# Moving the last group's norm over six stage joints and weight rounding one stage ahead

## The reference

```python
def _layernorm(x, axis=-1, eps=1e-05):
    m = jnp.mean(x, axis=axis, keepdims=True)
    v = jnp.var(x, axis=axis, keepdims=True)
    return (x - m) / jnp.sqrt(v + eps)
...
x = x + jnp.tanh(g_xattn[0]) * _L0_xattn_ref(_layernorm(x, axis=-1), ctx_1024, ctx_1024, ...)
x = x + jnp.tanh(g_ffn[0]) * _L0_ffn_ref(_layernorm(x, axis=-1), L0_ffn_w_q, ...)
x = x + jnp.tanh(g_xattn[1]) * _L1_xattn_ref(_layernorm(x, axis=-1), ctx_1024, _lenS2, ...)
x = x + jnp.tanh(g_ffn[1]) * _L1_ffn_ref(_layernorm(x, axis=-1), L1_ffn_W_base, ...)
x = x + jnp.tanh(g_xattn[2]) * _L2_xattn_ref(_layernorm(x, axis=-1), ctx_1024, ...)
x = x + jnp.tanh(g_ffn[2]) * _L2_ffn_ref(_layernorm(x, axis=-1), L2_ffn_gate_w, ...)
x = x + jnp.tanh(g_xattn[3]) * _L3_xattn_ref(ctx_1024, ctx_1024, _layernorm(x, axis=-1), mask, ...)
x = x + jnp.tanh(g_ffn[3]) * _L3_ffn_ref(_layernorm(x, axis=-1), L3_ffn_clip_x, ...)
```

```python
def _act_fake_quant(x, clip_factor):
    scale = jax.nn.sigmoid(clip_factor) * jnp.max(jnp.abs(x)) / QMAX
    return jnp.clip(_ste_round(x / scale), -QMAX - 1.0, QMAX) * scale

def _weight_fake_quant(w):
    scale = jnp.max(jnp.abs(w), axis=1, keepdims=True) / QMAX
    return jnp.clip(_ste_round(w / scale), -QMAX - 1.0, QMAX) * scale
xq = _act_fake_quant(x, clip_x[0])
gate = jnp.einsum('bsh,ih->bsi', xq, _weight_fake_quant(w_gate))
up = jnp.einsum('bsh,ih->bsi', xq, _weight_fake_quant(w_up))
h = _act_fake_quant(jax.nn.silu(gate) * up, clip_down[0])
return jnp.einsum('bsi,hi->bsh', h, _weight_fake_quant(w_down))
```

## Time and profile before

| | |
|---|---|
| median of 3 runs | 2173.85 us (2171.03 to 2174.78) |
| profiled execution, whole time | 2175.49 us |
| profiled execution, first to last instruction | 2173.7 us |
| mean granted TensorE clock, share of full speed | 0.930 |
| PE busy | 1925.7 us (89%) |
| DVE busy | 1558.8 us (72%) |
| ACT busy | 821.0 us (38%) |
| POOL busy | 729.3 us (34%) |

### The profile page before, as it was taken

One profiled execution on the slowest core, in us unless ns is written; L12 is line 12 of the kernel. 1 busy time (PEld: TensorE's weight loads), 2 busy tenths in 40 slices (PEclk: granted clock), 3 DMA queues, 4 the chain that ended last, 5 costly groups with the idle time before them and its releaser, 6 DMA issues. The chain is left out here.

```text
span 2173.7 us, 41664 instructions
## 1 busy us (share of the span) xinstructions
PE 1925.7 (89%) x14275; PEld 1026.0 (47%) x14275; DVE 1558.8 (72%) x3191; ACT 821.0 (38%) x1491; POOL 729.3 (34%) x967
## 2 busy tenths in 40 slices
PE   4659998998998987999999998969997999979965
PEld 2544444444444444555555554436663444436631
DVE  4767868878877865777777775756774666658978
ACT  3632012012012014666666663315652222225645
POOL 4551112112112105676666764454730000022301
PEclk8559999999999999999999998989998999999976
DMA  4302122122132141000000000000002533311001
GB/s 112 137 29 60 43 57 59 36 61 59 33 65 59 30 107 65 2 2 1 0 0 0 0 2 1 1 8 14 14 6 74 129 88 96 91 33 19 15 1 39
DMA packets 60079, 89.66 MB, mean 41 GB/s; under 512 B 23720, under 2 KB 42024, under 8 KB 55472
## 3 DMA queue, kind: packets, MB, share of 16 engines
q1 hardware_dynamic: 59952, 88.04, 16.5%
HBM read 80.85 MB, written 2.97 MB: 39 GB/s over the span
## 5 line engine op out<-in xcount | busy, mean ns | idle before, releaser
L916 POOL TENSOR_TENSOR l0f_v<-l0f_val,l0f_top 64x256 f32<-64x256 f32 x128 | 78.2, 611 | 488.4 <-DVE l0f_val L1191 479.9
L1021 PE MATMUL l0f_acc<-l0f_z,w_all 128*128 128x512 f32 x512 | 228.8, 609 | 15.0 <-DVE l0f_z L1229 15.0
L970 PE MATMUL l0f_work<-w_all,l0f_xs 128*128 128x512 f32 x384 | 183.5, 600 | 15.3 <-DVE l0f_val L1186 14.6
L241 POOL TENSOR_SCALAR var_eps<-mean_var 128x4 f32<-128x4 f32 (+1 forms) x64 | 14.6, 228 | 462.7 <-DVE mean_var L225 460.8
L1021 PEld LDWEIGHTS l0f_acc<-l0f_z,w_all 128*128 128x128 f32 x512 | 99.1, 195 | 144.0 <-issue 123.9
L1423 PE MATMUL l1x_proj_v<-l1x_wvo,l1x_cs 128*64 128x512 f32 x512 | 134.9, 605 | 0.1
L1191 DVE COPY_PREDICATED l0f_val<-l0f_oh,l0f_work 128x512 f32<-128x512 int32 x160 | 116.8, 730 | 23.7 <-PE l0f_work L970 7.5
L2828 DVE TENSOR_TENSOR l2f_hu<-l2f_act_g,l2f_pu 128x512 f32<-128x512 f32 x104 | 71.2, 684 | 66.8 <-ACT l2f_act_g L2754 65.4
L2754 ACT ACTIVATE l2f_act_g<-l2f_pg 128x512 f32<-128x512 f32 x104 | 61.5, 594 | 149.4 <-PE l2f_pu L2695 141.5
L2703 PE MATMUL l2f_acc<-l2f_hid,w_all 128*128 128x512 f32 x208 | 107.4, 598 | 10.3 <-DVE l2f_hid L2834 10.3
L2694 PE MATMUL l2f_pg<-xnT_all,w_all 128*128 128x512 f32 x208 | 108.7, 605 | 0.0
(11 more groups left out here) (389 smaller groups left out, 4418.6 us busy)
## 6 DMA issues: line engine op xcount, KB each, us to landing
l0f_first_mask<-onehots SPq DMA_DIRECT2D x32, 512.0 KB, 5.8
w_all<-onehots SPq DMA_DIRECT2D x32, 512.0 KB, 11.8
w_all<-combination SPq DMA_DIRECT2D x40, 256.0 KB, 5.0
w_all<-in_weights SPq DMA_DIRECT2D x1, 4640.0 KB, 16.7
l0x_m_b<-running_max SPq DMA_DIRECT2D x16, 256.0 KB, 4.5
w_all<-combination SPq DMA_DIRECT2D x16, 224.0 KB, 4.5
w_all<-combination SPq DMA_DIRECT2D x16, 192.0 KB, 4.1
w_all<-combination SPq DMA_DIRECT2D x16, 160.0 KB, 4.1
```

The source lines that it names most:

```text
L916: nc.gpsimd.tensor_tensor(v2[a * SEQ:(a + 1) * SEQ, t % 2, b, :, :], val[r, t % 2, :, :].rearrange("p (c a) k -> p c a k", a=2)[:, :, a, : ...
L970: nc.tensor.matmul(value_banks[e % 3][:, :], xs[:, t * P:(t + 1) * P], ve[:, e, :], start=True, stop=True).then_inc(ve_done, 1)
L1021: nc.tensor.matmul(acc[:, :], oe[:, n % E, n // E, :], z[:, n % Z, :], start=(n == 0), stop=(n == C * E - 1)).then_inc(acc_done, 1)
```

## The change

1. Six joints. The norm of the last group (two tiles at the joint from `l1_xattn` to `l1_ffn`) leaves the end of the stage and is done by the next one, under new names: `edge_measure` (statistics and means), `norm_gpsimd` and `norm_tensor` with the semaphores `EdgeSems`, `edge_apply`, `edge_scalar`. Each engine has them at a fixed place among the first steps of the next stage, and the steps that read the last group's `xnT`, or reuse the shared buffers, wait for `edge.ready` or `edge.turned`. The joint from the second narrow attention to `l3_ffn` keeps its norm where it is. The sets of semaphores have 53 members.
2. The block `late_weights` goes; its four loads are issued by SyncE in `l1_xattn`, behind the two loads of the lens.
3. The scales and the rounding of the weights of `l3_ffn` move into the last group of `l2_ffn` (steps 4, 5, 6 and 9 of 13), with buffers shared by the two stages (`Integers`), and with POOL's clearing of their padding.
4. In `l3_ffn` PE turns the rounded weights ahead of the spreading of the maximum, ACT copies them, and then has a small `Silu` of two values ahead of the first scaling. The clips of the input of groups 1 to 7 move from DVE to POOL; group 0's stay on DVE.

```diff
+def edge_measure(core, nc, dve, s, m=G):
+    dve.sem_inc(s.may_measure, 1)
+    for j in range(m):
+        norm_stats(core, nc, dve, s, TILES - m + j, j)
+    norm_means(core, nc, dve, s, 0, m)
...
+def edge_apply(core, nc, dve, s, m=G, tiles=None):
+    dve.wait_ge(s.rstd, count(1))
+    for j in tiles or range(m):
+        nc.vector.tensor_scalar(core.xn[:, 1, j, :], core.x[:, TILES - m + j, :], core.mv[:, j, 0:1], core.rs[:, j:j + 1],
+                                ALU.subtract, ALU.mult).then_inc(s.xn, 1)
...
+def edge_scalar(core, nc, act, s, bank, m=G):
+    act.wait_ge(s.turned, count(1))
+    nc.scalar.activation(core.xnT[:, (TILES - m) * P:TILES * P], bank[:, 0:m * P], ACT.Copy).then_inc(s.ready, 1)
...
-def late_weights(core, nc, d):
-    with nc.Block() as block:
-        @block.sync
-        def _(sp):
-            for i, (first, last) in enumerate(LOADS[4:]):
-                a, b = WEIGHTS[first][0], WEIGHTS[last][1]
-                sp.dma_start(core.w_all[:, a - LATE:b - LATE], d["weights"][:, a:b]).then_inc(core.w_loaded[4 + i], 16)
+def late_weights(core, sp, d):
+    for i, (first, last) in enumerate(LOADS[4:]):
+        a, b = WEIGHTS[first][0], WEIGHTS[last][1]
+        sp.dma_start(core.w_all[:, a - LATE:b - LATE], d["weights"][:, a:b]).then_inc(core.w_loaded[4 + i], 16)
...
-                    add_to_x(g)
+                    add_to_x(g, more)
                     if more:
                         softmax(g + 1, 0)
...
+                edge_measure(core, nc, dve, edge)
                 pick_experts(0)
+                edge_apply(core, nc, dve, edge)
                 pick(0, 0)
                 softmax(0, 0)
                 group(0, True, False)
+                dve.wait_ge(edge.turned, count(1))
                 with dve.Fori(1, GROUPS - 1) as g:
                     group(g, True)
                 group(GROUPS - 1, False)
-                norm_apply(core, nc, dve, ns, GROUPS - 1)
...
                     sp.dma_start(lens_i[b * SEQ:(b + 1) * SEQ, :],
                                  d["lens"][b:b + 1, :].broadcast_to([SEQ, TILES]))\
                         .then_inc(lens_loaded, 16)
+                late_weights(core, sp, d)
...
                         slot(g, j)
+                        if g == 0 and j == 1:
+                            norm_gpsimd(core, nc, pool, edge, 0)
+                pool.wait_ge(edge.ready, count(1))
                 with pool.Fori(2, GROUPS - 1) as g:
...
                         slot(g, j)
+                        if g == 0 and j == 3:
+                            pe.wait_ge(kT_ready, count(3))
+                            norm_tensor(core, nc, pe, edge, 0, turn1)
                 with pe.Fori(2, GROUPS - 1) as g:
...
                         slot(g, j)
+                        if g == 0 and j == 3:
+                            edge_scalar(core, nc, act, edge, turn1)
                 with act.Fori(2, GROUPS - 1) as g:
...
                         if g == 0 and j == 0:
                             key_masks()
+                            edge_measure(core, nc, dve, edge)
+                        if g == 0 and j == 2:
+                            edge_apply(core, nc, dve, edge)
                 with dve.Fori(2, GROUPS - 1) as g:
...
+                def weight_scales():
...
+                    for k in range(2):
+                        ch.link(nc.vector.tensor_reduce(ints.wsc[:, 0, 3 * k:3 * k + 3], w3[k], AX.X, ALU.max,
+                                                        apply_absolute_value=True))
+                    ch.link(nc.vector.tensor_reduce(ints.wsc[:, 0, 6:7], w3[2], AX.X, ALU.max, apply_absolute_value=True))
+                    ch.link(nc.vector.tensor_scalar(ints.wsc[:, 1, 0:7], ints.wsc[:, 0, 0:7], 1.0 / ints.QMAX, 1e-30,
+                                                    ALU.mult, ALU.max))
+                    ch.link(nc.vector.reciprocal(ints.wsc[:, 2, 0:7], ints.wsc[:, 1, 0:7]))
...
+                def round_weights(k):
+                    n = ints.I if k == 2 else ints.CH * P
...
+                    if k < 2:
+                        for c in range(ints.CH):
+                            ins = nc.vector.tensor_scalar(wq[:, c * P:(c + 1) * P], w3[k][:, c, :],
...
+                    else:
+                        ins = nc.vector.tensor_scalar(wq[:, 0:n], w3[2], ints.wsc[:, 2, 6:7], ints.MAGIC, ALU.mult, ALU.add)
+                    ch.link(ins)
+                    ch.link(nc.vector.tensor_scalar(wq[:, 0:n], wq[:, 0:n], ints.MAGIC, ints.QMAX, ALU.subtract, ALU.min))
+                    ch.link(nc.vector.tensor_scalar(ints.wq_bf[:, k, 0:n], wq[:, 0:n], -ints.QMAX - 1.0, None, ALU.max))
...
                             combine(g + 1)
+                    if g == GROUPS - 1:
+                        if c == 4:
+                            weight_scales()
+                        if c in (5, 6, 9):
+                            round_weights((5, 6, 9).index(c))
...
-                measure(GROUPS - 1)
-                norm_means(core, nc, dve, ns, GROUPS - 1)
-                norm_apply(core, nc, dve, ns, GROUPS - 1)
...
+                for g in range(1, GROUPS):
+                    pool.wait_ge(x_scaled, count(g + 1))
+                    nc.gpsimd.tensor_scalar(xr[:, g % 2, :], xr[:, g % 2, :], MAGIC + QMAX, MAGIC - QMAX - 1.0,
+                                            ALU.min, ALU.max).then_inc(x_clipped, 1)
+                    pool.wait_ge(x_clipped, count(g))
+                    after(pool, gu_done, (g - 1) * CH)
+                    nc.gpsimd.tensor_scalar(xq[:, g % 2, :], xr[:, g % 2, :], MAGIC, None, ALU.subtract)\
+                        .then_inc(xq_ready, 1)
                 pool.wait_ge(scales_ready, count(2))
...
+                pe.wait_ge(consts_ready, count(3))
                 for k in range(3):
-                    pe.wait_ge(wq_ready, count(k + 1))
                     for c in range(CH):
                         ins = nc.tensor.transpose(wbank[k][:, c * P:(c + 1) * P], wq_bf[:, k, c * P:(c + 1) * P],
                                                   core.ident_bf[:, :])
                     ins.then_inc(wt_done, 1)
+                spread_max_tensor(pe, 0)
                 pe.wait_ge(wT_ready, count(3))
...
+                act.wait_ge(consts_ready, count(3))
                 nc.scalar.activation(sig[:, :], clips, ACT.Tanh, scale=0.5).then_inc(sig_ready, 1)
-                act.wait_ge(scales_ready, count(1))
-                scale_x(0)
                 for k in range(3):
                     act.wait_ge(wt_done, count(k + 1))
                     nc.scalar.activation(wT[:, k, :], wbank[k][:, 0:CH * P], ACT.Copy).then_inc(wT_ready, 1)
+                nc.scalar.activation(sc[:, 16:18], clips, ACT.Silu).then_inc(gate_loaded, 1)
+                act.wait_ge(scales_ready, count(1))
+                scale_x(0)
...
                 nc.vector.tensor_reduce(mx[:, 0:1], core.x_max[:, :], AX.X, ALU.max)\
                     .then_inc(mx_ready, 1)
-                dve.wait_ge(core.w_loaded[7], 16)
-                ch.link(nc.vector.tensor_reduce(wsc[:, 0, 0:3], wgu[0], AX.X, ALU.max, apply_absolute_value=True))
-                ch.link(nc.vector.tensor_reduce(wsc[:, 0, 3:6], wgu[1], AX.X, ALU.max, apply_absolute_value=True))
                 own_max(0)
...
                 dve.wait_ge(sig_ready, count(1))
                 ch.link(nc.vector.tensor_scalar(sig[:, :], sig[:, :], 0.5, 0.5, ALU.mult, ALU.add))
                 spread_max(0)
                 ch.link(nc.vector.tensor_scalar(sc[:, SG:SG + 3], wsc[:, 1, 0:3], sc[:, SX:SX + 1], None, ALU.mult))
                 nc.vector.tensor_scalar(sc[:, SU:SU + 3], wsc[:, 1, 3:6], sc[:, SX:SX + 1], None, ALU.mult)\
```

234 lines of the change are left out of this document (161 added, 73 removed).

## The result

The changed kernel takes 2136.54 us (2133.39 to 2140.66, 4 runs) against 2172.44 (2169.21 to 2174.78, 4 runs) for the kernel before: a ratio of 0.983 with an interval of 0.9815 to 0.9845. The forecast was 2137.4. In a later set of runs the two stood at 2138.40 and 2178.26, ratio 0.9817 (0.9799 to 0.9834). The changed kernel's profiled execution spans 2138.6 us, 35.1 less than the 2173.7 of before.

A forecast was written before the change was run, and what follows sets the result against it. Uncovered latencies at the joints and DVE in `l3_ffn`'s loop were taken as bounds. Joints 32.9 plus `l3_ffn` 9.2, less costs 5.4 and rounding 0.2, save 36.5: 2173.85 becomes 2137.4, range 2129.5 to 2148.

The forecast's parts named there:

- The joints' gains: Six stage joints: uncovered time from last residual to last `xnT` copy goes, plus 2.2 for the load block; 32.9 us saved.
- the 3.5 priced from the other renewal and a barrier: End of `l0_xattn`: SyncE's semaphore renewal, priced from `l1_xattn`'s, stays bare, about 3.5 us after the residual; 2.8 saved.
- The costs behind the joints: Starts of the next stages: the moved norm work costs 5.4 us in sum; the ends could be 3 or 9.
- I had 2.8: Start of `l1_xattn`: measuring 1.4, applies 0.9 and PE 0.5 shift the DVE, POOL, DVE chain; bounds 1.4 and 4.0.
- the rival about the clock: Four joints: shorter gaps keep PE at the high clock, worth about 1.5 us each, so 2131; chance 0.13.
- Start of `l3_ffn`: First product at 2101.8 instead of 2106.44, through turned weights, scales, clips and gate; 4.6 us saved.
- the norm landing whole: Each joint: the moved norm costs 3.6 us on the bound engine instead of 0.9, so about 2152; chance 0.08.
- the slower case: `l3_ffn` loop: POOL's clips decide from 4.14 us a pair; slower overall from 10.0, then above 2174; chance 0.02.
- The rounding: Last group of `l2_ffn`: some 18 added DVE operations cost 0.2 us, bounds 0 and 2.
- POOL's clips: `l3_ffn` loop: POOL's pair takes 1.7 us, DVE stays the bound, groups fall from 4.80 to 4.14; seven save 4.6.
- the rival at 0.12: `l3_ffn` loop: POOL's clips hold DVE for their own length, the 4.6 us are lost, so 2142; chance 0.12.
- The table load: Start of `l3_ffn`: the 1.28 us load hides in the wait for scales; a drain would cut the gain to 3.6.

The follow-up runs named there:

- `joints_only`: Changed kernel with the old `l3_ffn`, no rounding in `l2_ffn` and the load block back: 2146.51 against 2178.26 for the kernel before, ratio 0.9855.
- `best`: Changed kernel with last-group norm work earlier in `l1_xattn` and SyncE's renewal in `l0_xattn` after the last decays: 2131.26 against 2177.36 for the kernel before.
- the padded kernel: Changed kernel with extra unread POOL clips in `l3_ffn`, one in groups 1 to 3, two in 4 to 7: 2140.39 against 2178.26 for the kernel before.
- the joint back: Changed kernel with the norm back in the tail of `l2_ffn`, no edge steps in the second narrow attention: 2141.60 against 2172.76 for the kernel before.
- delay: Changed kernel with POOL idling some 1.8 or about 3.6 us behind the last residual of `l2_ffn`: 2138.97 and 2140.61, one time each.

## Why the prediction was right, point by point

**The joints' gains.** The mechanism held wherever the residual was the last thing: 8.54, 4.38, 6.37, 5.78 and 6.36 became 0.50. Each of these gains is 0.2 to 0.3 smaller than its term, 1.2 in all, since the sum took the whole time up to the last copy as saved and so left 0.28 behind the residual, where 0.50 is left. The first joint kept SyncE's renewal, as the sum said, for 0.6 more than the 3.5 priced from the other renewal and a barrier. Together the joints gave 31.2 of 32.9.

**The costs behind the joints** were 5.4 in the sum. From start to last residual the seven stages ahead of `l3_ffn` grew by 4.3 together, rounding included, but with terms from -1.1 to +3.0. In `l1_xattn` the stage's residuals came 1.5 to 1.7 later, but its start had become 0.94 faster, since PE comes to it at the high clock (the mask's cast at 8.11 instead of 9.05 after the start). The work itself cost 2.5; in `joints_only`, with the load block still ahead and a low stretch from 0.2 to 7.0 us, the residuals but the last came 2.9 to 3.1 later, 0.5 of it since the cast waited for the load of the lens (9.52 instead of 9.05 after the start). I had 2.8. `best` has the same fast start and its second residual 0.5 ahead of the kernel before, so there the work cost 0.5, as PE's transposes were priced, and the rest was a matter of place: DVE waited 3.16 at the start, a wait that I named in the other stages and not here. In `l1_ffn` 0.2 instead of 0.7.

**What missed.** Seven stages miss their forecast by 0.6 or more: `l0_xattn`, `l2_ffn`, the second narrow attention and `l3_ffn` gave 5.1 less together, `l0_ffn`, `l1_xattn` and the first narrow attention 3.4 more. `l0_xattn` is the renewal. In `l0_ffn` the last residual came 1.0 earlier instead of 0.5 later, which no run explains. `l2_ffn` grew by 1.4 to its last residual instead of 0.7, less than the 2.2 between two executions of the kernel before. `l1_xattn` is its faster start, above. In the other three the granted clock differs where the time does. In the first narrow attention the last residual came 1.1 earlier instead of 0.5 later, in both traces of the change. In `l3_ffn` start and loop gave 4.67 and 7 x 0.67 = 4.7, as summed (4.6 and 4.6); the stage's last residual came 3.5 us after the last but two instead of 2.4, its last sets of four transposes taking 1.06 to 1.12 at the low level instead of 0.60 to 0.66, so 8.2 instead of 9.2. And the second narrow attention lost 3.0 instead of 0.4: the largest error of a term. The weakest step is the rival about the clock. It was priced with one sign, a gain of 1.5 at four joints through shorter gaps. That gain exists (0.9 in `l1_xattn`; `l1_ffn` is 119.9 instead of 122.4 long in three kernels in which the clock is high at its start), but losses exist as well, and far behind the joint. That the misses nearly cancel in the sum, 35.1 in the traces and 35.9 in the medians against 36.5, is luck in part; the range of 2129.5 to 2148 had room for either.

**Start of `l3_ffn`.** The 7.50 agree better than their terms. The terms as written add up to 2098.6 + 0.8 + 0.9 + 0.6 + 0.7 = 2101.6, not 2101.8. The scaling came 3.84 after the stage's start instead of 4.3, the nine transposes taking 1.14 instead of 1.5, and from the scaling to the first product were 3.66 instead of 3.0: the gate started 1.05 behind the first matmul's start, not 0.6.

**Two bounds** of the prediction are misreckoned, outside its range both: the norm landing whole would give 2137.4 + 16 = 2153, not 2152; and for the slower case the pairs must lose only what the other parts gain, 36.5 - 4.6 = 31.9, so it begins at 4.8 + 31.9 / 7 = 9.4 a pair, not 10.0.

**The rounding** at 0.2 was 0.0. **POOL's clips**: the pair is 2.1, not 1.7. The second clip was priced by a scaling with float32 output, 0.86, and takes 1.49; it still fits in 4.14, and the first takes only 0.61. That DVE doesn't pay, the rival at 0.12, is shown twice: 0.742 and 0.686 for its operations, as before, and groups 1 to 3 of the padded kernel unchanged. The Trainium skill ("SBUF — State Buffer", SBUF: two separate sides) says just this for DVE operations with one SBUF input and in no two-port mode; the trace agrees, with 0.74 at any time of POOL's operations. The slower case's first point, 4.14 a group, is borne out between 3.6 and 5.1; the pair of 2.1 is half of it.

**The table load.** The forecast had the gate 0.7 ahead of the first product and the load hidden between copies and scales; it ran from 2069.49 to 2070.77 and the scaling started at 2071.20, released by the scales. No drain behind the load is to be seen: the next activation started 0.01 later. By the Trainium skill's 1.4 of drain, an estimate from its figure ("ScalarE: Activation LUTs", What ACT_TABLE_LOAD costs) the scaling would have started near 2072.4, and the first product 8.7 after the stage's start instead of 7.50. The measurement decides. What I had missed is that the load needed no new place at all. In the old order it was the last thing ahead of the gate (2105.71, then 2105.72); with the weights turned first, the gate starts 6.78 after the stage's start whether or not the load stands before it.

## What to carry to other kernels

At a barrier between stages ask what is last on each queue, DMA and semaphore housekeeping too: the tail behind the last useful operation is gained when it moves, less what it costs in its new place, and only down to the next in line, which here ended 1.3 us (a copy) and some 3.8 us (the renewal) behind the residual. Put the moved work where the engine waits for something at the start of the next stage, not where its result is first wanted; a wait behind the new operation that is as long as before shows that the chain shifted and nothing was hidden. And a stage that an edit doesn't touch can change by 1 to 4 us with the granted clock, so claims of that size need stage lengths from several traces, and an undoing of the one edit.

## What the runs showed of the hardware that I had not expected

The granted clock in a stage's last groups differed with an edit 130 us ahead: 1.00 or 0.79 in the same code, 150.1 or 153.1 us. The attention took 150.1 and 151.1 before, 150.0 with `l3_ffn` alone changed and 150.1 with the joint back; it took 152.0 to 153.2 in six executions with the joint moved and no delay. One kernel broke the pattern, the padded one: its attention had the same program as the changed kernel's, its clock fell 146 us after the start, and it took 148.8. So the joint goes with the clock's place in ten of eleven executions without a delay, and doesn't decide it alone. POOL takes 1.49 us for a subtraction of 128x512 with bf16 output and 0.61 for a two-sided clip of the same size with float32 output, while DVE takes 0.43 for either.
